# A two-layer graph network on one core: what the node update stores, what the message pass streams, and who does the arithmetic of the last node pass

## The chip, the core and the metric

The kernel runs on one core of one Trainium2 chip. The metric is device time in microseconds. The core has TensorE (PE, with its weight loads PEld), VectorE (DVE), ScalarE (ACT), GpSimd (POOL) and the sync engine (SP), which issues most transfers; 16 DMA engines move the data. Indirect transfers (gathers and scatter-adds by an index) are issued by GpSimd.

## The reference, cut to what matters

There are 50000 nodes with 128 features and 25000 edges, sorted by destination. The part that the change touches is the second layer:

```python
x = x + L0(...)                          # s2 holds L0 before its relu, x the input: x2 = max(s2, 0) + x
h = maximum(_layernorm(x, axis=-1), 0)
# L1: messages over the edges
edge_input = concat([h[src], h[dst], edge_attr])
msg = layer_norm(relu(relu(edge_input @ eW1 + eb1) @ eW2 + eb2), eg, ebeta)
node_agg = segment_sum(msg, dst)
# L1: the nodes
upd = relu(concat([h, node_agg]) @ nW1 + nb1) @ nW2 + nb2
out = x2 + layer_norm(h + upd, ng, nbeta)
```

## The kernel before

Everything is float32. The 50000 nodes are worked on in 49 groups of 1024 rows (128 partitions x 8 tiles of 128 features, so 512 KB a group), the padded 25088 edges in 49 groups of 512. Seven passes run one behind the other, each a block in which every engine has its own instruction stream; semaphores order them. The first four are the relational layer. The change lies in the last three.

**Node update** (`node_pass_2`). For each group it loads s2 and x, forms x2 = max(s2, 0) + x on VectorE (L674) and stores it. VectorE takes mean and variance of each row (`Stats`: `bn_stats` on eight tiles, L147, then small instructions on 128x8, L154 to L188), ScalarE takes the root (L176). The normalised rows, three tiles on VectorE (L199) and five on ScalarE (L194), are transposed on TensorE (L789), pass a relu on ScalarE on their way out of PSUM (L748), are multiplied with nW1x (L803), copied out by ScalarE (L758) and stored as s3. Mean, deviation and shift of every row stay in SBUF until the last pass (`kept`). Meanwhile GpSimd gathers s2 rows for the edges ahead (L366).

**Message pass** (`edge_pass_messages`). For each group of 512 edges GpSimd gathers x2 at the destinations (L1476). VectorE forms x2 at the sources from gathered s2 and streamed x (L1514). All eight tiles get their row statistics (L147, L154 to L188); four are normalised on ScalarE (L194) and four on VectorE (L199). TensorE turns them (L1668) and two layers follow; the message is normalised on VectorE and multiplied with eg, plus ebeta (L1559, L1565). Equal destinations are added up by a matrix product, and GpSimd adds the sums to s3 by scatter (L1487). On GpSimd the order is: per group four gathers for three groups ahead and four scatters for the group before, two by two; a scatter waits until all scatters of the group before have landed.

**Last node pass** (`node_pass_3`). For each group it loads x2 and s3. ScalarE makes h from x2 with the kept statistics (L889, eight tiles). TensorE transposes s3 (L945), ScalarE adds nb1 and takes the relu (L900, two halves), TensorE adds bias (L959), h by the identity (L961) and the product with nW2 (L967) in PSUM, half by half. VectorE takes the statistics of the result out of PSUM (L147), ScalarE the root; five tiles are normalised by VectorE (L199), three by ScalarE (L194). GpSimd multiplies with ng (L996) and separately forms x2 + nbeta (L988), each on 1024 columns; VectorE adds the two in two halves (L1041), and SP stores the result.

In PSUM the transposes have two pairs of banks and the products two pairs. ScalarE's order in each step of the last pass is: hidden rows of the next group (both halves), h of the group after that, first four tiles, root for the group before, h last four tiles, normalising of the group before. Loops are `sweep`: the first four groups written out, then a hardware loop over four groups at a time, then the rest.

## Time and profile before

| | |
|---|---|
| time, median of 3 runs | 2980.29 us (2977.81 to 2980.57) |
| profiled execution, its own time | 2981.61 us |
| its span, first to last instruction | 2979.9 us |
| busy share of the span | PE 75%, DVE 71%, POOL 71%, PEld 64%, ACT 53% |
| mean granted clock of TensorE | 0.916 of full |
| moved by DMA | 473.22 MB, mean 159 GB/s |

The span is the time between the first and the last instruction of the profiled execution; its own time holds 1.7 us more around it. The shares are means over seven passes with different limits, so what one of them is worth is read inside its pass.

### The profile page before, as it was taken

The page shows a single profiled execution, that of the slowest core. Times are in us where ns is not written, and L with a number is a line of the kernel's source. Part 1 is how long each engine was busy: PE and PEld are TensorE (multiplying, and loading weights), DVE is VectorE, ACT ScalarE, POOL GpSimd, SP SyncE. Part 2 cuts the span into 40 slices and gives each one's busy share as a digit, 9 for nine tenths or more (in the row PEclk, how much of TensorE's full clock was granted, in tenths as well). Part 3 has the DMA queues.
Part 4 walks back from the last instruction along what each step waited for, and adds up shares of the span by engine and source line. Part 5 has one row for each costly group of instructions (what it writes and reads, how often), then busy time and mean ns, then how long its engine had stood idle before and what let it go on. Part 6 is the DMA issues. An engine that isn't in the chain of part 4 may idle for free. (4 is left out here: it accounts for less than half of the span.)

```text
span 2979.9 us, 56436 instructions
## 1 busy us (share of the span) xinstructions
PE 2220.2 (75%) x16219; PEld 1900.0 (64%) x16219; DVE 2123.9 (71%) x7295; ACT 1569.0 (53%) x3333; POOL 2117.5 (71%) x1577
## 2 busy tenths in 40 slices
PE   4779988888768898888845666577777777566765
PEld 4769888888667898888844565344444444354554
DVE  6978777677423586667627776677777777499999
ACT  4986555555423354444426776344444444476774
POOL 6775888888667288888857774688887777455555
PEclk9999999999889999999977888898999889799998
DMA  6985555555379645554529998444444443465663
GB/s 217 306 276 123 108 101 102 101 101 104 55 270 349 228 87 86 85 86 86 86 25 386 411 408 338 107 93 86 91 85 86 87 86 58 134 200 190 193 197 132
DMA packets 268196, 473.22 MB, mean 159 GB/s; under 512 B 62736, under 2 KB 142288, under 8 KB 268112
## 3 DMA queue, kind: packets, MB, share of 16 engines
q1 hardware_dynamic: 158352, 382.24, 38.8%
q0 software_dynamic: 109760, 90.00, 20.0%
q8 instruction: 35, 0.57, 0.1%
q14 instruction: 49, 0.40, 0.0%
HBM read 291.28 MB, written 180.81 MB: 158 GB/s over the span
## 5 line engine op out<-in xcount | busy, mean ns | idle before, releaser
L1149 POOL DMA_INDIRECT s<-E_summed,c_scat x392 | 658.8, 1681 | 207.3 <-issue 113.4
L1377 PE MATMUL ps<-c_w,E_masked 128*128 128x128 f32 x6272 | 738.0, 280 | 3.5 <-DVE E_masked L1180 3.4
L1377 PEld LDWEIGHTS ps<-c_w,E_masked 128*128 128x128 f32 x6272 | 730.0, 197 | 4.3 <-DVE E_masked L1180 4.3
L1180 DVE SCALAR_TENSOR_TENSOR E_masked<-E_type_row,E_hT 128x512 f32<-128x512 int32 x784 | 483.5, 687 | 79.9 <-ACT E_hT L1297 67.0
L366 POOL DMA_INDIRECT E_src_rows<-s,c_src x392 | 417.7, 1065 | 166.4 <-issue 118.0
L1487 POOL DMA_INDIRECT s<-E_summed,c_scat x196 | 322.5, 1646 | 100.6 <-issue 55.5
L1476 POOL DMA_INDIRECT E_ends<-x,c_near x196 | 199.9, 1020 | 95.2 <-issue 58.5
L1328 ACT COPY E_summed<-ps 128x512 f32<-128x512 f32 x98 | 57.4, 586 | 398.9 <-DMA s<-E_summed,c_scat 398.9
L366 POOL DMA_INDIRECT E_src_rows<-in_x,c_src x196 | 202.4, 1033 | 75.3 <-issue 60.3
L586 PE MATMUL ps<-c_sl,N_hT 128*128 128x128 f32 x1568 | 198.0, 281 | 18.4 <-DVE N_out L407 13.8
L1392 PE MATMUL ps<-E_msg,E_same 128*128 128x128 bf16 (+1 forms) x2450 | 207.3, 241 | 1.2 <-DVE E_msg L1230 1.2
L586 PEld LDWEIGHTS ps<-c_sl,N_hT 128*128 128x128 f32 x1568 | 186.2, 195 | 26.3 <-ACT N_hT L534 17.6
L1392 PEld LDWEIGHTS ps<-E_msg,E_same 128*128 128x128 bf16 (+1 forms) x2450 | 199.5, 136 | 1.9 <-DVE E_msg L1230 1.3
L572 PE MATMUL ps<-c_ident,N_xin 128*128 128x128 f32 x784 | 108.3, 283 | 112.7 <-POOL N_xin L199 43.4
L1307 ACT ACTIVATE E_same<-E_dst_row,c_dstf 128x128 f32<-128x128 int32 (+7 forms) x392 | 188.0, 554 | 1.9 <-DMA E_dst_row<-in_dst_line 1.9
L988 POOL TENSOR_TENSOR N_base<-N_xin,c_nbeta 128x1024 f32<-128x1024 f32 x49 | 115.2, 2351 | 99.0 <-DVE N_res L1041 88.1
L789 PE MATMUL ps<-c_ident,N_h 128*128 128x128 f32 x392 | 66.2, 323 | 152.0 <-ACT N_h L194 143.9
L996 POOL TENSOR_TENSOR N_res<-N_res,c_ng 128x1024 f32<-128x1024 f32 x49 | 117.6, 2400 | 83.6 <-DVE N_res L199 42.9
L407 DVE TENSOR_TENSOR N_out<-ps,c_b 128x512 f32<-128x512 f32 x98 | 63.2, 686 | 149.9 <-DMA s<-N_out 87.4
L889 ACT ACTIVATE N_h<-N_xin,c_x_shift,c_x_rstd 128x128 f32<-128x128 f32 x392 | 160.6, 491 | 17.8 <-DMA N_sin<-s 17.8
L572 PEld LDWEIGHTS ps<-c_ident,N_xin 128*128 128x128 f32 x784 | 90.4, 145 | 122.0 <-issue 80.8
L1680 PE MATMUL ps<-E_endsT,c_eW1s 128*128 128x512 f32 x98 | 75.4, 862 | 113.3 <-ACT E_edgeT L1605 113.3
(143 smaller groups left out, 4854.6 us busy)
## 6 DMA issues: line engine op xcount, KB each, us to landing
s<-N_out SPq DMA_DIRECT2D x147, 512.0 KB, 4.7
N_xin<-in_x SPq DMA_DIRECT2D x98, 512.0 KB, 5.5
N_sin<-s SPq DMA_DIRECT2D x98, 512.0 KB, 5.6
E_dst_row<-in_dst_line SPq DMA_DIRECT2D x147, 256.0 KB, 4.8
E_type_row<-in_type SPq DMA_DIRECT2D x98, 256.0 KB, 3.9
N_xin<-s SPq DMA_DIRECT2D x49, 512.0 KB, 6.4
x<-N_x SPq DMA_DIRECT2D x49, 512.0 KB, 11.6
N_xin<-x SPq DMA_DIRECT2D x49, 512.0 KB, 4.1
```

Source lines behind the costliest of these rows:

```text
L366: pool.indirect_dma_start(self.rows[:, at:at + D], None, table, bass.IndirectOffsetOnAxis(ap=self.index[:, self.issued:self.issued + 1], a ...
L572: ins = nc.tensor.transpose(ps[:, 2 * (u % 2) + k // 4, (k % 4) * P:(k % 4 + 1) * P], xin[:, u, k * D:(k + 1) * D], c["ident"][:])
L586: ins = nc.tensor.matmul(ps[:, 4 + 2 * (u % 2) + h, k * D:(k + 1) * D], hT[:, u % 2, at:at + P], w[:], start=True, stop=True)
L889: ins = nc.scalar.activation(h[:, u, cols], xin[:, u, cols], ACT.Relu, bias=c["x2_shift"][:, at], scale=c["x2_rstd"][:, at])
L996: nc.gpsimd.tensor_tensor(tiles_of(res[:, u, :]), tiles_of(res[:, u, :]), each_tile(c["ng"], NT), ALU.mult).then_inc(scaled, 1)
L1149: pool.indirect_dma_start(s, bass.IndirectOffsetOnAxis(ap=c["scat"][:, k:k + 1], axis=0), summed[:, g % 2, t * D:(t + 1) * D], None, compu ...
L1180: nc.vector.scalar_tensor_tensor(out=masked[:, u % 2, r, :], in0=type_row[:, u, :], scalar=float(r), in1=hT[:, u % 2, :], op0=ALU.is_equal ...
L1307: ins = nc.scalar.activation(same_block(same[:, u % 2, :], t, 0, t + 1), dst_row[:, u, 0:(t + 1) * P], ACT.Square, bias=c["dstf"][:, bass. ...
L1377: ins = nc.tensor.matmul(ps[:, 2 + u % 2, t * D:(t + 1) * D], masked[:, u % 2, r, t * P:(t + 1) * P], w[:, r, :], start=(r == 0 and t == 0 ...
L1392: ins = nc.tensor.matmul(ps[:, 4 + u % 2, t * D:(t + 1) * D], same_block(same[:, u % 2, :], s, t, t + 1), msg[:, u % 2, p, s * D:(s + 1) * D],
L1476: pool.indirect_dma_start(ends[:, u, GE + t * D:GE + (t + 1) * D], None, a["x2"], bass.IndirectOffsetOnAxis(ap=c["near"][:, k:k + 1], axis ...
L1487: pool.indirect_dma_start(a["s3"], bass.IndirectOffsetOnAxis(ap=c["scat"][:, k:k + 1], axis=0), summed[:, g % 2, t * D:(t + 1) * D], None, ...
```

## The change

The node update stores h, with its relu, in place of x2, and keeps no statistics. ScalarE normalises all eight tiles (with the relu), and VectorE copies the products out of PSUM in ScalarE's place. The message pass gathers h at the destinations, so that those four tiles need no statistics and no normalising. It also streams all node rows once: SP loads s2 and x of a node group, VectorE forms max(s2, 0) + x and adds nbeta in place, SP stores the sum as `base`. The last node pass loads s3, h and `base`; ScalarE normalises all eight output tiles, VectorE multiplies with ng and adds `base`, and GpSimd has no instruction there. Its products lie in a ring of three pairs of banks, its transposes in one pair. The last pass is written out for all 49 groups, with no loop. In its order below `residual` is the bias and h by the identity for one half, `update` the product with nW2, which waits for that half of the hidden rows; `halves` waits for the group's product and takes `bn_stats`, `scales` is reciprocal and shift, `scale` the product with ng and `finish` the sum with `base`, each on 512 columns.

```diff
 def node_pass_2
-                wait(sp, x2_ready, UNROLL * i + u - 3)
+                wait(sp, h_ready, UNROLL * i + u - 3)
                 sp.dma_start(sin[:, u, :], rows(a["s2"], node_base(i, u))).then_inc(loaded[u], 16)
                 sp.dma_start(xin[:, u, :], rows(a["x"], node_base(i, u))).then_inc(loaded[u], 16)
...
-                sp.wait_ge(x2_ready, g + 1)
-                sp.dma_start(rows(a["x2"], node_base(i, u)), x2[:, u, :]).then_inc(x2_stored[u], 16)
+                sp.wait_ge(h_ready, g + 1)
+                sp.dma_start(rows(a["h"], node_base(i, u)), h[:, u, :]).then_inc(h_stored[u], 16)
...
+            def results(i, u, half):
+                dve.wait_ge(product, 2 * g + half + 1)
+                nc.vector.tensor_copy(out[:, u % 2, half * 512:(half + 1) * 512],
+                                      ps[:, 4 + 2 * (u % 2) + half, :]).then_inc(out_ready, 1)
...
-                for k in range(NT - ON_ACT, NT):
+                wait(act, h_stored[u], 16 * i)
+                for k in range(NT):
                     cols = slice(k * D, (k + 1) * D)
-                    ins = ln.scaled(nc, h[:, u % 2, cols], x2[:, u, cols], k, g, ACT.Identity)
+                    ins = ln.scaled(nc, h[:, u, cols], sin[:, u, cols], k, u, ACT.Relu)
...
 def node_pass_3
+            def load(g):
+                wait(sp, product, 2 * (g - 3))
+                sp.dma_start(sin[:, u, :], rows(a["s3"], at(g))).then_inc(loaded[u], 16)
+                sp.dma_start(hin[:, u, :], rows(a["h"], at(g))).then_inc(loaded[u], 16)
+            def load_base(g):
+                wait(sp, out_ready, 2 * (g - 1))
+                sp.dma_start(base[:, u, :], rows(a["base"], at(g))).then_inc(based[u], 16)
...
         @block.scalar
+            def hidden_rows(g, half):
+                if half == 0:
+                    wait(act, product, 2 * (g - 1))
+                act.wait_ge(turned, 2 * g + half + 1)
+                nc.scalar.activation(hidT[:, g % 2, half * 512:(half + 1) * 512], ps[:, half, :], ACT.Relu,
+                                     bias=c["nb1"][:]).then_inc(hidT_ready, 1)
+            def outer_norm(g):
+                act.wait_ge(ln.shift_ready, g + 1)
+                wait(act, scaled_ready, 2 * (g - 1))
+                for k in range(NT):
+                    ins = ln.scaled(nc, normal[:, g % 2, k * D:(k + 1) * D], u_tile(g, k), k, g % UNROLL, ACT.Identity)
...
+            for g in range(GROUPS_N):
+                if g + 1 < GROUPS_N:
+                    hidden_rows(g + 1, 0)
+                ln.deviations(nc, act, c["eps"], g % UNROLL, g)
+                if g + 1 < GROUPS_N:
+                    hidden_rows(g + 1, 1)
+                outer_norm(g)
         @block.tensor
+            def turn(g):
+                pe.wait_ge(loaded[u], 32 * (g // UNROLL + 1))
+                wait(pe, hidT_ready, 2 * g)
+                for k in range(NT):
+                    ins = nc.tensor.transpose(ps[:, k // 4, (k % 4) * P:(k % 4 + 1) * P],
                                               sin[:, u, k * D:(k + 1) * D], c["ident"][:])
...
+            turn(0)
+            for g in range(GROUPS_N):
+                residual(g, 0)
+                if g + 1 < GROUPS_N:
+                    turn(g + 1)
+                residual(g, 1)
+                update(g, 0)
+                update(g, 1)
-        @block.gpsimd
...
         @block.vector
+            for g in range(GROUPS_N):
+                halves(g)
+                statistics(g)
+                if g:
+                    scale(g - 1, 0)
+                scales(g)
+                if g:
+                    scale(g - 1, 1)
+                    finish(g - 1, 0)
+                    finish(g - 1, 1)
...
 def edge_pass_messages
-    lx = Stats(sb, sem, "E3x", 2 * GT)
+    lx = Stats(sb, sem, "E3x", GT)
...
+            def load_base(i, u):
+                wait(sp, base_stored[u % 2], 16 * (2 * i + u // 2))
+                sp.dma_start(base[:, u % 2, :], rows(a["s2"], node_base(i, u))).then_inc(base_loaded[u % 2], 16)
+                sp.dma_start(base_x[:, u % 2, :], rows(a["x"], node_base(i, u))).then_inc(base_loaded[u % 2], 16)
+            def store_base(i, u):
+                sp.wait_ge(base_step, 2 * g + 2)
+                sp.dma_start(rows(a["base"], node_base(i, u)), base[:, u % 2, :]).then_inc(base_stored[u % 2], 16)
...
-                        ends[:, u, GE + t * D:GE + (t + 1) * D], None, a["x2"],
+                        ends[:, u, GE + t * D:GE + (t + 1) * D], None, a["h"],
...
-                for t in range(GT, 2 * GT):
-                    tile = ends[:, u, t * D:(t + 1) * D]
-                    ins = lx.normalise(nc.vector, tile, tile, t, u)
+            def update(i, u):
+                dve.wait_ge(base_loaded[u % 2], 32 * (2 * i + u // 2 + 1))
+                nc.vector.scalar_tensor_tensor(out=base[:, u % 2, :], in0=base[:, u % 2, :], scalar=0.0,
+                                               in1=base_x[:, u % 2, :], op0=ALU.max, op1=ALU.add).then_inc(base_step, 1)
+            def add_nbeta(i, u):
+                dve.wait_ge(base_step, 2 * (UNROLL * i + u) + 1)
+                nc.vector.tensor_tensor(tiles_of(base[:, u % 2, :]), tiles_of(base[:, u % 2, :]),
+                                        each_tile(c["nbeta"], NT), ALU.add).then_inc(base_step, 1)
...
                 if n:
-                    normalise(*n)
+                    scales(*n)
+                update(i, u)
                 message_variances(i, u)
                 message_norm(i, u)
+                add_nbeta(i, u)
...
-                pe.wait_ge(normed, g + 1)
+                pe.wait_ge(gathered[u], 64 * (i + 1))
```

## Rows read from the trace of the kernel before

**Rows 1.** Windows: us; busy PE, PEld, DVE, ACT, POOL; PEclk, DMA share, GB/s.
```profile
1560.00:1857.00 297.00, 178.71 (x1176) 168.64 (x1176) 218.77 (x980) 206.00 (x490) 205.11 (x184) 0.81 0.98 384
1857.00:2565.00 708.00, 499.77 (x2107) 294.68 (x2107) 494.98 (x2058) 285.07 (x638) 534.56 (x404) 0.89 0.45 84
2565.00:2980.00 415.00, 276.16 (x1470) 204.37 (x1470) 384.13 (x1127) 277.82 (x686) 232.74 (x98) 0.90 0.58 186
```

**Rows 2.** Windows, middle of the last node pass and of the message pass.
```profile
2600.00:2900.00 300.00, 208.20 (x1128) 154.16 (x1126) 294.23 (x855) 211.33 (x522) 175.31 (x75) 0.93 0.62 194
1900.00:2500.00 600.00, 447.67 (x1884) 262.94 (x1885) 443.80 (x1843) 253.57 (x569) 479.09 (x360) 0.90 0.47 87
```

**Rows 3.** Timeline of VectorE, first group of the last node pass: start, length.
```profile
2579.94 1.68 DVE L147 BATCH_NORM_STATS2 N_ln_st<-ps 128x6 f32<-128x128 f32 x8 [33.78 <-PE ps L967]
...
2582.30 0.17 DVE L169 TENSOR_TENSOR N_ln_var<-N_ln_small 128x8 f32<-128x8 f32 x1
```

**Rows 4.** Timeline of the last group's statistics in the last node pass.
```profile
2965.32 1.67 DVE L147 BATCH_NORM_STATS2 N_ln_st<-ps 128x6 f32<-128x128 f32 x8
```

**Rows 5.** Groups of GpSimd, message pass: count, busy us, mean ns, idle.
```profile
L1487 POOL DMA_INDIRECT s<-E_summed,c_scat x196 | 322.5, 1646 | 100.6 <-issue 55.5 <-ACT E_summed L1633 32.4 <-DMA s<-E_summed,c_scat 12.7
L1476 POOL DMA_INDIRECT E_ends<-x,c_near x196 | 199.9, 1020 | 95.2 <-issue 58.5 <-POOLq L618 35.8 <-DMA s<-E_summed,c_scat 0.9
L366 POOL DMA_INDIRECT E_src_rows<-s,c_src x12 | 12.1, 1009 | 3.7 <-issue 3.7
```

**Rows 6.** Waits of GpSimd in the message pass: total us, times, longest.
```profile
POOL s L1487 <- ACT E_summed L1633: 32.4, 6, 14.5
```

**Rows 7.** Groups of VectorE in the message pass.
```profile
L199 DVE TENSOR_SCALAR E_ends<-E_ends,E3x_ln_mean,E3x_ln_rstd 128x128 f32<-128x128 f32 x184 | 52.7, 364 | 0.0
...
L1565 DVE TENSOR_TENSOR E_normal<-E_scaled,c_ebeta 128x512 f32<-128x512 f32 x47 | 32.9, 701 | 1.6
```

**Rows 8.** Waits of VectorE in the message pass: total us, times, longest.
```profile
DVE E3x_ln_rstd L182 <- ACT E3x_ln_sd L176: 79.5, 48, 4.7
```

**Rows 9.** Groups of GpSimd in the node update.
```profile
L366 POOL DMA_INDIRECT E_src_rows<-s,c_src x160 | 178.1, 1113 | 48.8 <-issue 48.8
```

**Rows 10.** Timeline of GpSimd and VectorE in the node update.
```profile
1700.22 0.94 POOL L366 DMA_INDIRECT E_src_rows<-s,c_src  x1 [0.30 <-issue]
...
1701.27 1.23 DVE L674 SCALAR_TENSOR_TENSOR N_x<-N_sin,N_xin 128x1024 f32<-128x1024 f32 x1 [1.31 <-DMA N_xin<-in_x]
1701.47 1.85 POOL L366 DMA_INDIRECT E_src_rows<-s,c_src  x1 [0.30 <-issue]
```

**Rows 11.** DMA issues in the message pass: count, median us to landing.
```profile
E_ends<-x,c_near POOLq DMA_INDIRECT x196, 2.6
```

**Rows 12.** DMA issues in the node update: count, median us to landing.
```profile
E_src_rows<-s,c_src POOLq DMA_INDIRECT x160, 5.8
```

**Rows 13.** Timeline of ScalarE in the message pass, a deviation and what follows.
```profile
2202.70 0.30 ACT L176 ACTIVATE E3m_ln_sd<-E3m_ln_var,c_eps 128x4 f32<-128x4 f32 x1 [1.35 <-DVE E3m_ln_var L169]
2202.90 1.06 ACT L1604 ACTIVATE E_endsT<-ps 128x512 f32<-128x512 f32 x2
```

**Rows 14.** Groups of ScalarE in the last node pass.
```profile
L900 ACT ACTIVATE N_hidT<-ps,c_nb 128x512 f32<-128x512 f32 x88 | 55.9, 696 | 0.0
L194 ACT ACTIVATE N_res<-ps,N_ln_shift,N_ln_rstd 128x128 f32<-128x128 f32 x135 | 52.1, 454 | 58.4 <-DVE N_ln_shift L188 58.4
```

**Rows 15.** Timeline of TensorE's weight loads and matmuls in the last node pass.
```profile
2702.65 0.10 PEld L959 LDWEIGHTS ps<-c_nb_parts,c_parts_weight 96*128 96x128 bf16 x1
...
2703.84 1.05 PE L967 MATMUL ps<-c_nW,N_hidT 128*128 128x128 f32 x8
...
2704.62 0.91 PEld L945 LDWEIGHTS ps<-c_ident,N_sin 128*128 128x128 f32 x8
```

**Rows 16.** Windows of 3.4 us in the last node pass.
```profile
2706.40:2709.80 3.40, 0.90 (x3) 0.60 (x4) 3.40 (x11) 2.19 (x6) 1.95 (x2) 1.00 0.27 47
2709.80:2713.20 3.40, 3.40 (x12) 2.43 (x11) 3.33 (x12) 2.27 (x8) 1.46 (x1) 0.51 1.01 327
```

More of the change, by code:

```diff
@@ L696, in both @@
[L696 to L708 removed]
+                ln.halves(nc, [sin[:, u, k * D:(k + 1) * D] for k in range(NT)])
@@ L710, in step @@
             def step(i, u):
                 if first(i, u):
-                    updated(0, 0)
-                    halves(0, 0)
-                    ln.sums(nc, dve, 0)
-                    ln.means(nc, dve, 0, 0)
-                    ln.totals(nc, dve, 0, 0)
-                    both((0, 1), (0, 0))
-                    both((0, 2), (0, 1))
+                    for k in range(3):
+                        updated(0, k)
+                        halves(0, k)
+                        ln.sums(nc, dve, k)
+                        ln.means(nc, dve, k, k)
+                        ln.totals(nc, dve, k, k)
+                        if k < 2:
+                            scales(0, k)
@@ L719, in step @@
                 n, m = ahead(i, u, 3), ahead(i, u, 2)
                 if n:
-                    both(n, m)
-                elif m:
-                    reciprocals(*m)
-                    ln.shifts(nc, UNROLL * m[0] + m[1])
-                    normalise(*m, range(NT - ON_ACT)).then_inc(normed, 1)
+                    updated(*n)
+                if m:
+                    scales(*m)
+                if n:
+                    g = UNROLL * n[0] + n[1]
+                    halves(*n)
+                    ln.sums(nc, dve, g)
@@ new lines, in load_base, with store @@
+            def load_base(g):
+                u = g % 2
+                wait(sp, out_ready, 2 * (g - 1))
+                sp.dma_start(base[:, u, :], rows(a["base"], at(g))).then_inc(based[u], 16)
+            def store(g):
+                u = g % 2
+                last_store(sp, stored, g)
+                sp.wait_ge(out_ready, 2 * g + 2)
+                sp.dma_start(rows(a["out"], at(g)), res[:, u, :]).then_inc(stored[u], 16)
+            for g in range(UNROLL):
+                load(g)
@@ L877, in _ @@
+            for g in range(2):
+                load_base(g)
+            for g in range(GROUPS_N):
+                if g + 4 < GROUPS_N:
+                    load(g + 4)
+                if g >= 1:
+                    store(g - 1)
+                    if g + 1 < GROUPS_N:
+                        load_base(g + 1)
+            store(GROUPS_N - 1)
+            all_stored(sp, stored)
         @block.scalar
         def _(act):
-            LOWER, UPPER = range(0, NT // 2), range(NT // 2, NT)
-            def rows_h(i, u, tiles):
-                g = UNROLL * i + u
-                act.wait_ge(loaded[u], 32 * (i + 1))
-                wait(act, product, 2 * (g - 3))
-                for k in tiles:
-                    cols = slice(k * D, (k + 1) * D)
-                    at = bass.ds(g * NT + k, 1)
-                    ins = nc.scalar.activation(h[:, u, cols], xin[:, u, cols], ACT.Relu,
-                                               bias=c["x2_shift"][:, at], scale=c["x2_rstd"][:, at])
-                ins.then_inc(h_ready, 1)
@@ new lines, in update @@
+            def update(g, half):
+                pe.wait_ge(hidT_ready, 2 * g + half + 1)
+                for k in range(4):
+                    hid = half * 512 + k * P
+                    ins = nc.tensor.matmul(u_bank(g, half)[:, k * D:(k + 1) * D], hidT[:, g % 2, hid:hid + P],
+                                           c["nW2"][:], start=False, stop=True, skip_group_check=True)
+                ins.then_inc(product, 1)
+            turn(0)
+            for g in range(GROUPS_N):
+                residual(g, 0)
+                if g + 1 < GROUPS_N:
+                    turn(g + 1)
+                residual(g, 1)
+                update(g, 0)
+                update(g, 1)
@@ L1066, in edge_pass_relational @@
+            for half in range(2):
+                scale(GROUPS_N - 1, half)
+            for half in range(2):
+                finish(GROUPS_N - 1, half)
 def edge_pass_relational(nc, sb, sem, c, ps, a, name, x, s, w, norm, gathers):
@@ L1572, in step @@
                     variances(0, 0)
[L1573 removed]
+                    scales(0, 0)
                 n = ahead(i, u, 1)
```

350 lines of the change are left out of this document (112 added, 238 removed).

## Prediction

> **What bounds the kernel now.** I read the windows of the passes first, since the change touches three of seven: node update, message pass and last node pass take 297, 708 and 415 us of 2979.9 [rows 1]. They have three different limits.
>
> The node update is limited by transfers: DMA share 0.98, and no engine above 219 of 297 us [rows 1]. The last node pass is limited by VectorE, busy 294.2 of 300 us in its middle [rows 2]. From the first group's statistics (2579.94) to the last's (2965.32) there are 48 steps: 385.4 / 48 = 8.03 us each [rows 3, 4].
>
> The message pass is the one to look at twice. No engine is at its limit by busy time. But GpSimd issues 404 indirect transfers there, 322.5 + 199.9 + 12.1 = 534.5 us, and before each stands 0.3 us of "issue", 117.7 us in sum: 652 us of work [rows 5]. Between its first and last transfer it waits only 32.4 us for sums to scatter (14.5 of them once, for the first group) and 13.6 us for transfers: 698 us [rows 5, 6]. So GpSimd alone needs 652 / 49 = 13.3 us a group, and the chain through VectorE, ScalarE and TensorE, for which it waits the other 18 us, about 0.4 more. Two limits lie almost on top of each other, and GpSimd has 18 us in hand for the whole pass.
>
> **Node update.** The bytes stay: two loads and two stores of 512 KB a group, h in place of x2. VectorE loses three normalising instructions (3 x 0.36 = 1.1 us) and gains two copies of 128x512, by the nearest row 0.70 each [rows 7]: +0.3 us a group on 218.8 / 49 = 4.5, against 297 / 49 = 6.1 [rows 1]. ScalarE gives those copies away and takes three more tiles, about even. The transfers cover both. A load now waits for h instead of x2, some 6 us later (2.5 us of statistics, then 0.3 and eight tiles on ScalarE); its slot comes back after four groups of 6 us, so I take 0. At DMA share 0.98 there is nothing to gain; above, I allow 10 us for loads that come late.
>
> **Message pass.** Removed from VectorE in each group: four statistics (half of 1.68 us [rows 3]) and four normalising instructions (52.7 / 184 x 4 = 1.1 us [rows 7]). Added: two instructions of 128x1024 with two inputs in SBUF. The trace has one such, 1.23 us [rows 10]; I take it for both. The first stands where the normalising instructions stood: 1.23 for 1.1, even. The second stands between the message's norm and the next source rows: 1.23 - 0.84 = +0.4 us ahead of a reciprocal which today waits 79.5 / 48 = 1.66 us for ScalarE [rows 8]. Where that cover is short it costs up to 0.4. TensorE's turn still waits for ScalarE's tiles. I leave the chain where it is.
>
> The price is on GpSimd. In the node update one gather starts at 1701.47, inside the instruction of 1701.27 to 1702.50, and takes 1.85 us where its neighbour takes 0.94; the mean is 1.113 [rows 9, 10]. With four gathers to each such instruction it costs (1.113 - 0.94) x 4 = 0.69 us. That is the upper end: in the message pass GpSimd starts a transfer every 1.6 us, not every 1.4. The lower end comes from the gathers of that pass, 0.08 longer than 0.94, with three two-input instructions of 512 columns in each group: 4 x 0.08 / 3 = 0.11 for each, and by the square of the length (chance to be hit times mean rest) 0.11 x (1.23 / 0.70)^2 = 0.33. I take 0.55, nearer to the 1024-column row: 2 x 0.55 x 49 = 54 us. GpSimd then needs 652 + 54 + 14.5 + 13.6 = 734 us for what took 698: +36. The ends give 652 + 32 + 28 = 712 (+14) and 652 + 68 + 28 = 748 (+50); nothing only if every one falls between two starts.
>
> The Trainium skill (GPSIMD Engine Reference, Key points) says that GpSimd's SBUF interfaces are shared with VectorE and contended by instructions with two SBUF inputs or in a two-port mode. The first half is what the row shows. By the second half the four normalising instructions that go would have held it as well, and would give back 4 x 0.36^2 / (2 x 1.6) = 0.16 us a group, 8 us in all, +28 in place of +36. No row separates them, and the sum leaves it out.
>
> SP gets three more transfers of 512 KB a group. The DMA share is 0.47 here [rows 2]; 1.5 MB at the node update's 384 GB/s [rows 1] is 4 us of 13.7, so about 0.76. SP's queue is: loads of edges, store of the last sum, wait for its landing, two loads of the next; the loads land some 12 us into a step and are wanted about 20 us into it. Hidden. What can suffer is GpSimd's wait for its own scatters: gathers land in 2.6 us here, and in 5.8 where the DMA is full [rows 11, 12]. Between nothing and 3.2 us a group I take nothing, since the DMA stays short of full, and keep 1.5 for a rival.
>
> **Last node pass.** Removed: eight ScalarE tiles of h, GpSimd's two operations, five normalising instructions on VectorE. Added: ScalarE's three output tiles become eight, and VectorE gets two products of 512 columns. VectorE's work is then 1.68 + 0.85 + 0.4 + 4 x 0.70 = 5.7 us [rows 3, 7], ScalarE's 2 x 0.69 + 0.3 + 8 x 0.39 = 4.8 [rows 13, 14]. By busy time the pass would fall from 8.03 to about 6.
>
> But the new order makes a ring. ScalarE does for each group: first half of the next hidden rows, deviation of this group, second half of the next hidden rows. TensorE's turn waits for both halves of the group before, since the transposes have one pair of banks. So the deviation of group g, which needs product g, stands ahead of the turn, and product g+1 stands behind that turn. Around the ring:
> - statistics, 2579.94 to the end of the variance at 2582.47: 2.53 us [rows 3];
> - deviation: the next ScalarE instruction starts 0.20 behind its start [rows 13], and 0.04 for the hop;
> - hidden rows, second half: 0.69 [rows 14], and 0.04;
> - TensorE: eight transposes 0.93 (one weight load each, 0.91 in all); a half with bias, identity and update 1.97, from 2702.65 to 2704.62; eight more update instructions 1.05, and 0.25 until the last has drained [rows 15]: 4.2 us;
> - hop to VectorE: 0.08.
> The sum is 7.78 us at full clock, 0.25 below today's step.
>
> The clock takes that back. TensorE idles from the end of the early bias and identity (1.1 us behind the product) until the turn (3.5 us behind it): 2.4 us in each group. The granted clock fell to its lower level (1.2 GHz) at 2709.8, after TensorE had been busy for 0.90 of 3.40 us, and was back at 2.4 GHz by 2713.2 [rows 16]. Today that is off the path; in the ring each low stretch lies on it. The mean is 0.93 of full in this pass and 0.90 in the message pass, where TensorE also waits inside the chain [rows 2]. I take the latter: the lost work is 0.10 of the period, T = 7.78 + 0.10 T, T = 8.64. Bounds: 7.78 with the clock always full, and 9.7 with the node update's 0.81 [rows 1].
> The first statistics come no earlier, as the first turn waits for the same two loads. The end is shorter: ScalarE's eight tiles and four VectorE instructions behind the last statistics give about 12 us to the end of the span, against 14.6 now [rows 4]: -2.6. So 48 x (8.64 - 8.03) - 2.6 = +27 us, between -15 and +78.
>
> **Sum.** 0 + 36 + 27 = +63 on the profiled execution's own 2981.6 (its span and 1.7 around it): 3044.6. It lies 1.3 above the median of the runs, so 3043.
>
> **Rivals.**
> - GpSimd's delays hide, last pass as above: +27, 3007. For it: its transfers are not much longer than 0.94 today. Against: the 18 us in hand are used up by 0.37 us a group. 0.12.
> - TensorE keeps its clock in the ring: last pass -15, message pass +36: 3001. For it: the idle stretch is shorter than the pass has today. Against: the message pass's mean clock. 0.10.
> - Faster: the last pass runs at the pace of its busiest engine, 5.7 us, say 5.9 with hops: 48 x (5.9 - 8.03) = -102, with the message pass -66: 2914. It decides if the second hidden half is ready without the deviation in front of it. Against: both stand in order on one engine. The Trainium skill (GPSIMD Engine Reference, Key points) holds VectorE to be about twice as fast as GpSimd at elementwise work; who goes by that alone expects this case. 0.08. Another 0.05 goes to full clock and hidden delays together: -15, 2965.
> - Scatters land later behind the new transfers, 1.5 us a group: +74 more, 3117. 0.07.
>
> **How the numbers follow.** My forecast has the remaining 0.58. Its own range: message pass +14 to +50, last pass at a clock of 0.93 (8.37 us, +14) to 0.85 (9.15 us, +51): 3008 to 3081. The range leaves out the late scatters and the two faster cases (0.20 together), takes in 3007 and 3001 and the node update's 10: 2996 to 3088. A measurement here tells 0.2% (6 us) from no change. Faster 0.13, slower 0.84, and 0.03 for the ground between the cases.
>
> **What would show it.** Message pass: GpSimd's mean transfer 0.1 us longer or more, its waits for sums gone but for the first, the pass near 744 us. Last pass: statistics 8.4 to 8.9 us apart, VectorE busy about two thirds and waiting for TensorE's product in each group, TensorE's turn waiting for the hidden rows, a mean clock near 0.9. I am wrong if VectorE does not wait for the product (then there is no ring), or if GpSimd's transfers keep their length.

## The result and the profile after

The changed kernel takes 3058.78 us (median of 4 runs, 3048.54 to 3061.82), the kernel before beside it 2980.43 us (2977.81 to 2987.26). The ratio is 1.0253, 95% interval 1.0223 to 1.0283: slower by 78 us. The forecast was 3043 us, range 2996 to 3088. The profiled execution is the longest of the four: 3061.82 us, span 3060.1, against a span of 2979.9.

The windows of the three passes after the change, columns as in [rows 1]: length, busy time of the five engines, clock, DMA share, GB/s.
```profile
1557.00:1857.00 300.00, 177.52 (x1176) 167.31 (x1176) 238.76 (x931) 222.91 (x539) 208.26 (x186) 0.81 0.96 381
1857.00:2645.00 788.00, 527.57 (x2107) 305.39 (x2107) 517.83 (x1765) 285.56 (x637) 551.92 (x404) 0.84 0.63 174
2645.00:3061.00 416.00, 278.72 (x1470) 200.72 (x1470) 250.65 (x980) 213.41 (x539) 0.00 (x0) 0.90 0.70 248
```
The node update keeps its length (300 us for 297). The message pass goes from 708 to 788 us. The last node pass keeps its length although GpSimd has nothing left to do in it and VectorE is busy 134 us less.

Marks inside the passes say it more exactly. These are two rows of VectorE's statistics, of the messages and of the last node pass: count, duration min/median/max, start of the first and of the last instruction.
```profile
L146 DVE BATCH_NORM_STATS2 E3m_ln_st<-E_msg x196: 274/276/296, 1886.1 to 2611.8; 128x6 f32<-128x128 f32 x196
...
L146 DVE BATCH_NORM_STATS2 N_ln_st<-ps x392: 276/279/300, 2657.4 to 3050.1; 128x6 f32<-128x128 f32 x196
```
In the kernel before the same two rows run from 1888.2 to 2541.9 and from 2579.9 to 2966.7. So of the 80.2 us in the spans
- -2.1 lie ahead of the first message,
- +72.0 between the first message and the last (725.7 us for 653.7: 15.1 us a group for 13.6),
- +7.6 between the last message and the first product of the last pass (45.6 for 38.0),
- +5.9 in the last pass (8.15 us a group for 8.03),
- -3.2 behind the last statistics.

**Message pass.** GpSimd's groups from 1900 to 2500, to be read against [rows 5]: busy us, mean ns, idle and what ended it.
```profile
L1432 POOL DMA_INDIRECT s<-E_summed,c_scat x154 | 258.0, 1675 | 126.4 <-ACT E_summed L1587 86.9 <-issue 37.0 <-DMA s<-E_summed,c_scat 2.2
L1421 POOL DMA_INDIRECT E_ends<-h,c_near x154 | 168.7, 1095 | 46.9 <-issue 46.9
```
The same 600 us of the kernel before:
```profile
L1487 POOL DMA_INDIRECT s<-E_summed,c_scat x176 | 290.6, 1651 | 78.1 <-issue 50.9 <-ACT E_summed L1633 14.5 <-DMA s<-E_summed,c_scat 12.7
L1476 POOL DMA_INDIRECT E_ends<-x,c_near x174 | 178.6, 1027 | 53.0 <-issue 52.4 <-DMA s<-E_summed,c_scat 0.6
```
The means were 1651 and 1027 ns. Eight transfers and eight gaps of 0.3 now take 4 x (1.675 + 1.095) + 2.4 = 13.48 us a group, before 13.11: the two added VectorE instructions hold GpSimd for 0.37 us a group, not for the 1.10 that the sum had. What has grown is idle time: 86.9 us of "waiting for ScalarE's copy", 31 times (12.0 of them once, for the first group's sums; before, that one wait was 14.5 and the only one). ScalarE itself waits there; the waits of the same 600 us (total, times, longest):
```profile
POOL s L1432 <- ACT E_summed L1587: 86.9, 31, 12.0
...
ACT E_summed L1587 <- DMA s<-E_summed,c_scat: 73.5, 27, 5.2
```
The kernel before has no such wait of ScalarE. One such step, in the timelines of GpSimd, ScalarE's copy of the sums, and SyncE's queue:
```profile
2219.05 1.63 POOL L1432 DMA_INDIRECT s<-E_summed,c_scat  x1 [0.30 <-issue]
2220.98 2.32 POOL L1432 DMA_INDIRECT s<-E_summed,c_scat  x1 [0.30 <-issue]
2223.61 1.01 POOL L1421 DMA_INDIRECT E_ends<-h,c_near  x1 [0.31 <-issue]
2224.93 0.98 POOL L1421 DMA_INDIRECT E_ends<-h,c_near  x1 [0.30 <-issue]
2228.83 1.62 POOL L1432 DMA_INDIRECT s<-E_summed,c_scat  x1 [2.92 <-ACT E_summed L1587]
...
2228.05 0.58 ACT L1587 COPY E_summed<-ps 128x512 f32<-128x512 f32 x1 [5.17 <-DMA s<-E_summed,c_scat]
...
2219.37 0.33 SPq L1385 DMA_DIRECT2D E_base<-s  x1
2219.80 0.38 SPq L1386 DMA_DIRECT2D E_base_x<-in_x  x1
2220.79 0.33 SPq L1377 DMA_DIRECT2D E_xsrc<-xsrc  x1
2221.32 0.38 SPq L1378 DMA_DIRECT2D E_edge<-in_edge  x1
2221.89 0.36 SPq L1380 DMA_DIRECT2D E_dst_row<-in_dst_line  x1
```
The last scatter of a group is issued by 2223.30. Two gathers follow until 2225.91. Then GpSimd waits until 2228.83: 5.53 us from the end of one group's last scatter to the next group's first, of which two gathers with their gaps fill 2.9. In the same microseconds SyncE has put five loads into the DMA engines, and the windows around it show them full until 2227 and empty behind:
```profile
2216.00:2221.50 5.50, 5.50 (x28) 3.70 (x27) 5.28 (x19) 2.21 (x5) 4.59 (x4) 1.00 0.63 161
2221.50:2227.00 5.50, 1.50 (x12) 1.26 (x12) 1.94 (x11) 1.38 (x4) 3.80 (x3) 0.97 1.05 324
2227.00:2233.00 6.00, 2.69 (x3) 1.18 (x4) 4.03 (x9) 2.21 (x5) 3.56 (x3) 0.50 0.14 14
```
One name in these rows misleads. The view puts GpSimd's wait down to ScalarE's copy, which ended last. But the scatters at 2228.83 are the 22nd group's, and the copy at 2228.05 is the 23rd's (counted from the start of the pass). By the code the scatters of group g-1 need the copy of g-1, done a step earlier at 2211.12, and the landing of group g-2; the copy of g needs the landing of g-2 too, since there are two buffers of `summed`. Both wait for the same landing. The updates of the scatters' semaphore in the trace say so too: in 32 groups in the middle (the 10th to the 41st) the copy starts 0.02 us behind the last update, and the scatter 0.8 us behind it, as GpSimd also does after a landing in the kernel before, where ScalarE waits for none. From the end of a group's last scatter to that update it is 4.7 us in the mean here and 2.2 in the kernel before; in the 4 us behind the last scatter the share of the DMA engines is 1.1 here and between 0.3 and 0.6 before.

**Last node pass.** TensorE's timeline, with the wait that the prediction names:
```profile
2808.41 1.06 PE L900 MATMUL ps<-c_ident,N_sin 128*128 128x128 f32 x8 [2.54 <-ACT N_hidT L870]
...
2812.39 1.02 PE L912 MATMUL ps<-N_hin,c_ident 128*128 128x512 f32 x2
2815.95 1.06 PE L900 MATMUL ps<-c_ident,N_sin 128*128 128x128 f32 x8 [2.54 <-ACT N_hidT L870]
```
TensorE's turn waits 2.54 us for the hidden rows in each group, and the waits from 2700 to 3000 show the two other legs of the ring:
```profile
ACT N_ln_sd L175 <- DVE N_ln_var L168: 137.9, 36, 4.8
...
DVE N_ln_st L146 <- PE ps L920: 107.2, 36, 4.0
PE ps L900 <- ACT N_hidT L870: 93.9, 37, 2.5
```
The step is 7.54 us where the clock stays full (2808.41 to 2815.95). Apart from the last one (5.2 us, with no turn behind it) the 48 steps are of two kinds, 28 of 7.54 or 7.55 us and 19 of 9.20. The windows of one of each show the clock:
```profile
2804.80:2812.40 7.60, 5.06 (x32) 3.67 (x32) 5.14 (x21) 4.35 (x11) 0.00 (x0) 1.00 0.61 214
2812.40:2821.60 9.20, 6.66 (x32) 4.75 (x31) 5.10 (x21) 4.35 (x11) 0.00 (x0) 0.81 0.79 284
```
In the longer kind TensorE's work takes 1.6 us more at a clock of 0.81, and the step grows by as much. The mean is 8.15.

### The profile page after: what moved, and what is told of

The parts are those of the page before. It is cut to its first block and busy times, and to the rows that moved or that the text cites. A ratio compares the mean times of both kernels' runs of the same rounds, so it can differ in the third digit from the quotient of the medians.

```text
span 3060.1 us, 54163 instructions
## 1 busy us (share of the span) xinstructions
PE 2250.5 (74%) x16219; PEld 1907.4 (62%) x16219; DVE 2033.5 (66%) x6805; ACT 1521.7 (50%) x3235; POOL 1904.1 (62%) x1479
## 5 line engine op out<-in xcount | busy, mean ns | idle before, releaser
L1421 POOL DMA_INDIRECT E_ends<-h,c_near x196 | 211.6, 1080 | 92.2 <-issue 59.4
L146 DVE BATCH_NORM_STATS2 N_ln_st<-ps 128x6 f32<-128x128 f32 x392 | 82.3, 281 | 181.2 <-PE ps L920 181.2
L193 ACT ACTIVATE N_h<-N_sin,N_ln_shift,N_ln_rstd 128x128 f32<-128x128 f32 x392 | 156.1, 481 | 19.0 <-DVE N_ln_shift L187 18.6
L900 PE MATMUL ps<-c_ident,N_sin 128*128 128x128 f32 x392 | 53.5, 281 | 147.0 <-ACT N_hidT L870 119.3
```

Source lines behind the costliest of these rows:

```text
L146: ins = nc.vector.bn_stats(self.st[:, k, :], tiles[k])
L193: return nc.scalar.activation(out, in_, func, bias=self.tile(self.shift, slot, k), scale=self.tile(self.rstd, slot, k))
L1421: pool.indirect_dma_start(ends[:, u, GE + t * D:GE + (t + 1) * D], None, a["h"], bass.IndirectOffsetOnAxis(ap=c["near"][:, k:k + 1], axis= ...
```

## The experiments

Nine kernels, each beside runs of the kernel before on the same chip. "Against before" is the difference of the two medians; the changed kernel has +78.4 there.

| kernel | median us | against before | ratio, 95% interval | first to last message | step of the last pass |
|---|---|---|---|---|---|
| changed | 3058.78 | +78.4 | 1.0253 (1.0223 to 1.0283) | 725.7 | 8.15 |
| no base transfers | 3023.64 | +43.8 | 1.014 (1.012 to 1.016) | 684.7 | 8.19 |
| no base arithmetic | 2982.77 | +2.9 | 1.0007 (0.9997 to 1.0017) | 652.9 | 8.19 |
| hidden halves ahead | 2948.65 | -31.2 | 0.9898 (0.988 to 0.9916) | 720.5 | 5.80 |
| gathers ahead | 2984.62 | +4.7 | 1.0015 (1.0006 to 1.0025) | 654.7 | 8.19 |
| both orders | 2864.20 | -118.1 | 0.9615 (0.9597 to 0.9633) | 652.8 | 5.80 |
| filler | 3026.78 | +44.5 | 1.0157 (1.0132 to 1.0183) | 722.2 | 7.50 |
| three sums | 3021.87 | +39.5 | 1.0141 (1.0121 to 1.0161) | 685.1 | 8.15 |
| base behind copy | 2987.80 | +5.5 | 1.0026 (1.0015 to 1.0038) | 655.6 | 8.19 |
| before, gathers ahead | 2978.53 | +2.9 | 1.0011 (1.0001 to 1.0021) | 652.0 | 8.02 |

The two last columns come from the two statistics rows shown above, of each trace; a step is the distance of first and last start, less 1.4 us (the eighth instruction of a group begins 1.4 behind the first), by 48.

### No base transfers

```diff
-                    load_base(0, 0)
+                    load_base(0, 0); load_base(0, 1)
...
-                if l: store_base(*l)
-                if m: load_base(*m)
...
-                dve.wait_ge(base_loaded[u % 2], 32 * (2 * i + u // 2 + 1))
+                dve.wait_ge(base_loaded[u % 2], 32)
+                wait(dve, base_step, 2 * (UNROLL * i + u - 1))
...
-   rows(a["base"], at(g))
+   rows(a["x"], at(g))
```

> The changed kernel without the transfers of base in the message pass: s2 and x are loaded for the first two groups only, both VectorE instructions stay and work on those two buffers, nothing is stored, and the last node pass loads the same number of bytes from x. (The output so lacks the base sum.) Theory A, the scatters land later because 1.5 MB more a group is moved: the step of the message pass goes back from 15.1 us to 13.6, -65 to -80 us in all, with the last scatter's landing back inside 2.9 us and no wait of ScalarE's copy of the sums for it. Theory B, the prediction's own term, GpSimd is held by the two VectorE instructions: they are all still there, so the pass keeps +36 us of its +72, and no more than 36 come back; GpSimd's means stay at 1.67 and 1.08 us.

3023.64 us: 35 us come back, half of what theory A (late landings by traffic) expected, and as many as theory B (GpSimd held) allowed. But B's own account doesn't fit either. GpSimd's groups from 1900 to 2500:
```profile
L1427 POOL DMA_INDIRECT s<-E_summed,c_scat x163 | 272.6, 1672 | 99.3 <-ACT E_summed L1583 51.1 <-issue 39.9 <-DMA s<-E_summed,c_scat 8.3
L1416 POOL DMA_INDIRECT E_ends<-h,c_near x162 | 174.8, 1079 | 49.4 <-issue 49.1 <-DMA s<-E_summed,c_scat 0.3
```
It still waits 47 us for landings (51.1 and 8.3, less 12.0 for the first group's sums), with no transfer of base in the pass. The gap from a group's last scatter to the next first one is 4.39 us in the mean over 32 groups in the middle, against 5.47 in the changed kernel and 3.28 in the kernel before; the landing comes 3.5 us behind the end of the last scatter, against 4.7 and 2.2.

### No base arithmetic

```diff
-                sp.wait_ge(base_step, 2 * g + 2)
+                sp.wait_ge(base_loaded[u % 2], 32 * (2 * i + u // 2 + 1))
+                sp.wait_ge(normal_ready, g + 1)
...
-                update(i, u)
...
-                add_nbeta(i, u)
```

> The changed kernel with all transfers of base, and without the two 1024-column VectorE instructions; the store waits for the loads and for the message's norm, so that it leaves at about the same time. (What is stored is s2 alone.) Theory A, late landing: the message pass stays near 15 us a step, 0 to -12 us in all. Theory B, GpSimd held by these instructions: -36 us, between -14 and -50, with GpSimd's means down to 1.65 and 1.02 us.

2982.77 us: 75 us come back. Theory A had 0 to -12, theory B at most -50; both are wrong. The transfers alone cost nothing. GpSimd's groups:
```profile
L1433 POOL DMA_INDIRECT s<-E_summed,c_scat x176 | 287.1, 1632 | 79.5 <-issue 50.4 <-DMA s<-E_summed,c_scat 17.3 <-ACT E_summed L1586 11.8
L1422 POOL DMA_INDIRECT E_ends<-h,c_near x174 | 177.9, 1022 | 53.1 <-issue 50.6 <-DMA s<-E_summed,c_scat 1.5 <-PE ps L1624 0.9
```
With the same 1.5 MB a group the gap is 3.38 us. So lateness belongs neither to the traffic nor to the VectorE instructions by themselves. What separates the traces is how far GpSimd runs behind. From the timelines of ScalarE and GpSimd, the start of a group's first scatter less the start of the copy of its sums, in us:

| group | before | no arithmetic | gathers ahead | no transfers | changed |
|---|---|---|---|---|---|
| 5th | 5.4 | 6.8 | 6.1 | 7.2 | 8.6 |
| 11th | 10.2 | 10.2 | 14.3 | 16.9 | 16.3 |
| 25th | 4.7 | 4.3 | 12.7 | 15.8 | 16.7 |
| 41st | 3.1 | 5.2 | 10.1 | 15.2 | 16.1 |

GpSimd falls behind in the first ten groups in all of them, because each has one gather of source rows more (10 in these 600 us; 1.3 us with its gap, so 14.4 a group in place of 13.1 in the kernel before). How far it may fall behind follows from the two buffers. The copy of group g finds its buffer free if g-2 has landed: the lag, 10.2 us (first scatter of a group to the end of its last, the mean of 32 groups; 11.4 in the step shown above) and a landing of 2.2 must fit into two of the chain's steps of 13.6 us, so by this estimate the lag may be some 15. Before, and without the arithmetic, the lag stays under it and shrinks again, since GpSimd's 13.1 us are less than the chain's 13.6. In the changed kernel the lag passes it in the ninth group; from then on the chain steps with GpSimd.

That gave **theory C**: GpSimd, slower by some 0.4 us a group, fills both buffers; from then on it and the chain run in a fixed phase, and in that phase SyncE's loads of each group fall on the landing of its last scatter, which two gathers no longer cover. The kernel before shows the same collision singly: loads at 2224.75 to 2226.21, a last scatter until 2227.90, the next one at 2231.94 after 1.43 us of waiting, 11 times in 600 us.

### Gathers ahead

```diff
                 for q in range(2):
                     if g + 3 < GROUPS_E:
                         gather(g + 3, q)
+                for q in range(2):
                     if g > 0:
                         scatter(g - 1, q)
```

> The changed kernel, in the message pass GpSimd issues all four gathers of group g+3 ahead of the four scatters of group g-1, in place of two and two. The same transfers and instructions. Theory A, landing of the last scatter ahead of the next group's first: four gathers with their issue gaps (5.4 us) now cover a landing of 4.3 to 5.0 us where two (2.7 us) did not, so the step goes from 15.1 to between 13.6 and 14.0 us: -50 to -72 us. Theory B, GpSimd held: the order changes nothing, 0 to -10 us. A third case, where ScalarE's copy of the sums sets the step with the landing: -20 to -40 us.

2984.62 us: 74 come back, with all instructions and transfers in place. That is about theory A's number, but C gives it as well: four gathers and their gaps take 4 x 1.079 + 5 x 0.3 = 5.8 us, and cover a landing in whichever phase. The scatters of a group also take 7.7 us in the mean in place of 10.2 (7.4 in the 11th, 2048.65 to 2056.04), so that GpSimd may fall further behind before it holds both buffers, some 17 us by the same estimate; its lag of 14.3 does no harm. GpSimd's groups, 1900 to 2500:
```profile
L1432 POOL DMA_INDIRECT s<-E_summed,c_scat x175 | 295.5, 1689 | 64.5 <-issue 53.0 <-ACT E_summed L1588 11.5
L1421 POOL DMA_INDIRECT E_ends<-h,c_near x172 | 185.6, 1079 | 52.4 <-issue 48.5 <-DMA s<-E_summed,c_scat 4.0
```
The means are as long as in the changed kernel, or longer. Against the kernel without the arithmetic they are 0.057 us longer each: 8 x 0.057 = 0.46 us a group is the price of the two instructions, and it is hidden here.

### Base behind copy

```diff
             def load_base(i, u):
+                wait(sp, summed_ready, UNROLL * i + u - 1)
                 wait(sp, base_stored[u % 2], 16 * (2 * i + u // 2))
```

> The changed kernel; in the message pass SyncE issues the two loads of base, and with them the loads of edges queued behind, only when ScalarE has copied the sums (some 7 us later than now). The same bytes, instructions and buffers. Theory C: the loads then run at the start of GpSimd's round and not at its last scatter, the gap behind that falls from 5.5 to about 3 us, the step from 15.1 to near 13.8: -45 to -70 us. Rival, GpSimd's pace or the amount of traffic sets the step: 0 to -10 us. If the loads come too late for VectorE's update, the pass gets longer: +10 to +50.

2987.80 us: 73 come back for one wait on SyncE. The timeline of a step, GpSimd's last scatter and the next group's first, then SyncE's loads:
```profile
2291.49 2.31 POOL L1433 DMA_INDIRECT s<-E_summed,c_scat  x1 [0.30 <-issue]
2294.10 1.01 POOL L1422 DMA_INDIRECT E_ends<-h,c_near  x1 [0.30 <-issue]
2295.42 0.98 POOL L1422 DMA_INDIRECT E_ends<-h,c_near  x1 [0.30 <-issue]
2296.71 1.62 POOL L1433 DMA_INDIRECT s<-E_summed,c_scat  x1 [0.30 <-issue]
...
2282.48 0.33 SPq L1386 DMA_DIRECT2D E_base<-s  x1
...
2284.74 0.36 SPq L1380 DMA_DIRECT2D E_dst_row<-in_dst_line  x1
...
2296.32 0.33 SPq L1386 DMA_DIRECT2D E_base<-s  x1
```
The loads now run at the start of a step, and the DMA windows have moved with them: share 0.89 in the 5.5 us from 2282.5, 0.34 in those around the last scatter.
```profile
2282.50:2288.00 5.50, 3.55 (x8) 1.31 (x9) 5.00 (x12) 2.20 (x5) 4.58 (x3) 1.00 0.89 267
2291.00:2296.50 5.50, 2.38 (x20) 1.92 (x18) 3.05 (x13) 3.07 (x8) 4.49 (x4) 1.00 0.34 45
```
In the 4 us behind the last scatter the share is 0.4 over 32 groups, and the landing comes 1.8 us behind its end, for 4.7 in the changed kernel. The gap is 2.97 us in the mean, just the two gathers. The lag stays at 14.5 us (25th and 41st group), and ScalarE's copy waits for the landing 34 times in the 600 us:
```profile
ACT E_summed L1588 <- DMA s<-E_summed,c_scat: 50.0, 34, 4.1
```
So the chain still steps with GpSimd, but GpSimd's step is now its own work, 4 x (1.742 + 1.079) + 2.4 = 13.7 us. This is the run that separates the two parts: being tied to GpSimd costs 1.9 us from the first message to the last (655.6 for 653.7), the collision costs the other 70. What stays of the tie is 7.9 us behind the last message (45.9 us to the first product, for 38.0).

### Three sums

```diff
-    scaled = sb("E3_scaled", [P, GE])
+    scaled = msg
-    summed = sb("E3_summed", [P, 2, GE])
+    summed = sb("E3_summed", [P, 3, GE])
...
-                wait(act, scaled_step, 2 * g)
+                wait(act, normal_ready, g)
...
-                wait(act, added, 64 * (g - 1))
-                nc.scalar.copy(summed[:, u % 2, :], ...
+                wait(act, added, 64 * (g - 2))
+                nc.scalar.copy(summed[:, g % 3, :], ...
```

> The changed kernel with three buffers of summed in place of two in the message pass (to make room, the scaled messages are written over the messages, and ScalarE's loop is written out). Theory C, after the first four runs: GpSimd needs some 0.4 us a group more, falls behind until it holds both buffers, and from then on the chain steps with GpSimd, in a phase where the loads of a group fall on the landing of its last scatter. With a third buffer the chain is held later or not at all, and the gap from a last scatter to the next first one stays near the 2.9 to 3.5 us that two gathers cover: -30 to -55 us. Rival: landings are late with this traffic whatever the phase, so GpSimd keeps its 15.1 to 15.7 us a group: 0 to -12 us.

3021.87 us: 39 come back, inside C's -30 to -55. (With the shared buffer ScalarE's message also waits a little longer, `normal_ready` for `scaled_step`; no run takes that apart.) The gaps are 3.87 us in the mean, between 3.0 and 3.6 in most steps and over 5 in every fourth or so. ScalarE's copy is held no more; the lag settles near 18 us, and what is late next is a gather, for which TensorE's turn waits (2100 to 2500):
```profile
PE ps L1622 <- DMA E_ends<-h,c_near: 35.8, 13, 4.3
...
POOL s L1432 <- DMA s<-E_summed,c_scat: 20.8, 11, 2.6
```
So the third buffer moves the place where GpSimd's lateness is felt and takes away half of the price, no more.

### Hidden halves ahead

```diff
                 if g + 1 < GROUPS_N:
                     hidden_rows(g + 1, 0)
-                ln.deviations(nc, act, c["eps"], g % UNROLL, g)
-                if g + 1 < GROUPS_N:
                     hidden_rows(g + 1, 1)
+                ln.deviations(nc, act, c["eps"], g % UNROLL, g)
                 outer_norm(g)
```

> The changed kernel, in the last node pass ScalarE issues both hidden halves of group g+1 ahead of the deviation of group g. Theory of the ring (deviation between the halves sets the step): the step falls from 8.15 us to between 6.1 and 6.6, that of the 2 MB a group at 384 GB/s with hops (5.5) or of VectorE's 5.7 us plus its waits: -75 to -98 us. Rival, the pass is bound by its transfers of 2 MB a group or by VectorE already: 0 to -10 us.

2948.65 us: 110 come back, more than the 98 expected at most, since the step falls to 5.80 us. The window 2700 to 2900 and ScalarE's timeline of one group:
```profile
2700.00:2900.00 200.00, 172.19 (x1038) 125.72 (x1037) 174.80 (x682) 149.69 (x381) 0.00 (x0) 1.00 0.97 360
```
```profile
2801.61 1.30 ACT L870 ACTIVATE N_hidT<-ps,c_nb 128x512 f32<-128x512 f32 x2
2803.47 0.30 ACT L175 ACTIVATE N_ln_sd<-N_ln_var,c_eps 128x8 f32<-128x8 f32 x1 [0.57 <-DVE N_ln_var L168]
2804.39 2.90 ACT L193 ACTIVATE N_normal<-ps,N_ln_shift,N_ln_rstd 128x128 f32<-128x128 f32 x8 [0.62 <-DVE N_ln_shift L187]
```
Both hidden halves now stand ahead of the deviation. TensorE keeps its full clock, and the pass runs against VectorE (0.87 busy) and the transfers (share 0.97) at once.

### Filler

```diff
+                for _ in range(7 if half == 0 else 1):
                     nc.tensor.matmul(u_bank(g, half), c["parts_weight"][:], ..., start=True, stop=False)
```

> The changed kernel; in the last node pass TensorE computes the first half's bias product seven times instead of once (each overwrites the one before, the result is the same), so that it is idle 1.2 us instead of 2.5 in each group of the ring. If the granted clock of the ring is what separates the mean step of 8.15 us from the 7.55 us measured at full clock: every step at 7.55, -25 to -30 us, and a granted clock of 1.0 in the pass. If the step is made of the chain's own work whatever the clock: 0. If the extra products lie on the ring: +10 to +60.

3026.78 us: 34 come back by giving TensorE more work (the expectation had 25 to 30; 31 of the 34 are the last pass, 48 x (8.15 - 7.50)). The window of the pass:
```profile
2660.00:3010.00 350.00, 292.63 (x1670) 196.13 (x1668) 238.06 (x934) 201.80 (x510) 0.00 (x0) 1.00 0.78 271
```
The granted clock is 1.00 throughout, where the same window of the changed kernel has 0.92. Every step but the last is 7.55 us (7.50 in the mean): that is the ring's own length, and 0.65 us a group was the clock's.

### Both orders

The edits of "gathers ahead" and "hidden halves ahead" together.

> The changed kernel with both reorderings together: four gathers ahead of the four scatters in the message pass, and both hidden halves ahead of the deviation in the last node pass. They lie in different passes. If they add up: -74 and -110 us, so about 2875 us (2862 to 2888), faster than the kernel before by 3.5%. If the shorter message pass only moves a wait into the last pass: 2900 to 2945.

2864.20 us, ratio 0.9615 (0.9597 to 0.9633): the fastest of all, 118 us under the kernel before. Its two statistics rows:
```profile
L146 DVE BATCH_NORM_STATS2 E3m_ln_st<-E_msg x196: 272/277/296, 1877.0 to 2529.8; 128x6 f32<-128x128 f32 x196
...
L146 DVE BATCH_NORM_STATS2 N_ln_st<-ps x392: 275/280/300, 2572.7 to 2852.5; 128x6 f32<-128x128 f32 x196
```
Each pass is as long as with its own edit alone (652.8 us and 5.80 a step). It is 13 us faster than the sum of the two; 9 of them lie ahead of the first message (1877.0 for 1886.1), in stages that have the same instructions in the changed kernel and all its variants. No run explains those 9; the first message of the variants starts anywhere from 1877.0 to 1889.5.

### Before, gathers ahead

The same edit of GpSimd's order in the kernel before.

> The kernel before, with the one reordering of GpSimd in its message pass: four gathers ahead of four scatters. Its chain is not held by GpSimd in the middle of the pass, where two gathers already cover the landing, so the order is worth 0 to -6 us there. If the kernel before already loses time to landings of scatters: -15 to -40 us, and the gain of the reordered changed kernel would not be the change's.

2978.53 against 2975.61 us, ratio 1.0011 (1.0001 to 1.0021): no gain. The landings that the order hides are lost only where the change has made them late.

## Why the prediction was right, and where not

The forecast, slower and 3043 us, came out: 3058.78, inside the range and inside the forecast's own 3008 to 3081. That it came so near is in part luck. Each of its two terms lies outside its own range, and the errors have opposite signs: message pass +36 (+14 to +50) against +79.6 (72.0 and 7.6 at its end), last pass +27 (+14 to +51) against +2.7 (5.9 and -3.2). In the message pass the forecast had the engine right and not what it loses its time with; in the last pass the ring is as forecast, and only its sizes are off.

- **Node update, 0:** as forecast; the first message comes 2.1 us earlier, less than the traces differ among themselves there.
- **VectorE's chain, nothing:** as forecast. With the two instructions and the landings covered the pass is 654.7 us, without them 652.9.
- **GpSimd held, +36:** the hold is there, but 0.37 to 0.46 us a group where the sum had 1.10, under its lower bound of 0.66 (0.29 without the transfers of base, 0.57 with base behind copy). The sign that the prediction named, a mean transfer 0.1 us longer or more with the waits for sums gone, did not come: the means are 0.024 and 0.068 us longer, and the waits grew. The term was sized by the node update's rows [rows 9, 10], from which a 1024-column instruction costs 0.69; here it costs some 0.2. The Trainium skill (SBUF — State Buffer, Who interferes with whom) says that a VectorE instruction with two SBUF inputs contends with a GpSimd instruction that reads SBUF. By that rule these transfers, whose row numbers lie in SBUF, would be held, and the 0.057 us on each agree with it. The same section infers that a `tensor_tensor`, which one of the two instructions is, leaves GpSimd's writing of DMA descriptors alone; no run here shows through which port the hold comes. The other rule that the prediction weighed, that the normalising instructions had held GpSimd too (8 us back), stays open: without them and the arithmetic GpSimd's means are 0.019 and 0.005 us shorter than before, 0.10 us a group or 5 us in all, but four statistics left with them.
- **The step that failed:** "Between nothing and 3.2 us a group I take nothing, since the DMA stays short of full". The mean share did stay short of full, 0.63 for the pass; the step looked at the mean, where the moment counts. In the 4 us behind each group's last scatter the engines are full (a share of 1.1 over 32 groups, with 0.3 to 0.6 before), and that scatter lands 4.7 us behind its end instead of 2.2. The Trainium skill (DMA: Bandwidth & Descriptors, Issuing engines are not separate DMA queues) has the rule: transfers from whichever queue run on the same 16 engines and interleave. The trace agrees: scatters from GpSimd's queue that leave a gap of 2.6 us in the quiet end of the pass (2609.07 to 2611.66, with no gather between) leave 5.5 beside SyncE's loads.
- **How the two add up:** the prediction treated hold and landing as separate terms, and the first four runs refuted each of them alone. From the first message to the last the arithmetic alone costs 31.0 us (684.7 for 653.7), the transfers alone -0.8, both together 72.0. The hold by itself is 49 x 0.37 = 18 us, just the 18 us that GpSimd had in hand, and where the landings are covered or early it costs 1.0 us (gathers ahead, 654.7) or 1.9 (base behind copy, 655.6). So nearly all of the 72.0 are landings that came into the open once both buffers were full. The 31.0 are most likely the same (the landing comes 3.5 us behind the last scatter there); no run takes them apart. The rival "scatters land later" (+74) had the right place and nearly the size, 70. The forecast's +36 had its sign from a hold that in itself costs 1 to 2 us; but without the hold the landings cost nothing either.
- **+7.6 at the end of the pass** was in no term. The last pass reads the sums of all groups, and GpSimd's last scatter ends 26.8 us behind the last message, for 18.2 before.
- **Ring in the last pass:** shown. Statistics, deviation, second hidden half, turn and product wait for one another in each group; putting the deviation behind both halves breaks the ring and gives the 5.8 us a step that the rival "busiest engine's pace" had at 5.9. That rival's condition, the second half ahead of the deviation, was the right one.
- **Ring's length, 7.78 us:** 7.54. **Clock, 0.86 us a group:** 0.65. The formula, the missing clock charged to the whole step, holds: 7.54 at a clock of 0.92 gives 8.20, and the mean of all steps but the last is 8.22; a step at 0.81 is 9.20 long. What was mis-sized are the two numbers in it, the ring by 0.24 us and the clock, 0.90 taken from the message pass where these steps have 0.92. (The prediction's upper bound of 9.7 at 0.81 should read 7.78 / 0.81 = 9.6, and its +78 then +73; nothing else rests on it.)
- **Tail, -2.6:** -3.2.

Not settled: why the gap in the fixed phase is 4.4 us without the transfers of base and 5.5 with them. The smaller burst (0.64 MB of edge data a group in place of 1.7) ends sooner, which fits: the share is 0.83 and 0.58 in the first and second 2 us behind the last scatter, where the changed kernel has 1.1 in both. But no run changed the size of the burst alone.

## What to carry to other kernels

A queue that has a little time in hand can absorb a small slowdown or a burst of transfers, and not both: ask how far it may fall behind (buffers times step, less its own round and landing), and what phase it is held in once that is used up. A mean DMA share says little about a transfer on whose landing something waits; look at the half step around it, and move the burst or put other work behind the last scatter. When work is taken off the busiest engine, look in each engine's written order for an instruction that waits for this group and stands ahead of one that the next group needs: moving one ScalarE instruction took 110 us off here, where the whole change had added 78.

## What the hardware showed that was not expected

- Landing of a group's last indirect scatter, from the end of GpSimd's instruction: 1.8 us where the DMA share behind it is 0.4 (base behind copy), 4.7 beside 1.7 MB of loads from another queue at a share of 1.1, with the same instructions on GpSimd. The next scatter, when it waits for nothing else, starts 0.8 us behind the landing.
- Two VectorE instructions of 128x1024 with two SBUF inputs (1.22 us each) lengthened GpSimd's indirect transfers by 0.057 us each in the message pass, 0.46 us a group. In the node update the prediction put 0.69 us of longer gathers down to one such instruction; the DMA share is 0.98 there, and no run tells the two apart.
- Six useless matmuls a group (1.3 us of TensorE, in a wait of 2.5) made the last pass 31 us shorter: the granted clock rose from 0.92 to 1.00, and the steps of 9.20 us were gone.
